# Roots at the head of the step, the FFN bias and the joining of statistics on Vector

## The chip, the cores and the metric

One core of one Trainium2 chip. The metric is the device time of one execution in microseconds, lower is better. The kernel before takes 4009.88 us (median of three runs, 4008.35 to 4010.98).

## What is computed

Sixteen images of 96 channels and 96 x 96 pixels go through two layers. Layer 0 normalises each pixel over its channels, cuts the image into 3 x 3 patches, and for each patch finds the row of a 512 x 96 table and the pixel that match best (a score divided by the pixel's norm); the chosen row, the chosen pixel and the nine similarities of that row go through a small MLP and a convolution and are added to x. A quantised feed-forward network (FFN, 96 to 384 to 96) on the normalised pixels is added to that. Layer 1 divides each normalised pixel by (2 + 1e-4 y)^0.75, where y is the sum of squares over a 5 x 5 window, adds this to x, and adds a second FFN. The part that matters here:

```
def _qlinear(x, W, b):
    y = q_acc(jnp.einsum('bsk,nk->bsn', q_mul(x), q_mul(W)))
    return q_acc(y + q_mul(b))          # q_acc rounds to 10 mantissa bits
def _ln_c(v, eps=1e-6):                 # _gn and _ln_t: the same form, eps 1e-5
    m = jnp.mean(v, axis=1, keepdims=True)
    s = jnp.var(v, axis=1, keepdims=True)
    return (v - m) / jnp.sqrt(s + eps)
```

## The kernel before, in words

A tile is 128 patches (on the partitions) of J = 9 pixels of C = 96 channels; an image is SLOTS = 8 tiles, and there are NT = 128. The kernel is one software pipeline written by hand. In step k each stage works on another tile, by the offsets of `PARTS`: fs (k+4) loads a tile and takes its statistics, f1 (k+3) scores it and selects the pixel, f2 (k+2) finds the table row, f3 (k+1) is the MLP, the convolution and the residual x1, back (k) and tail (k-1) are the first FFN, root2 (k-2) keeps what layer 1 needs, columns and pre (k-10, k-11) apply the window factors, rear and rtail (k-12, k-13) are the second FFN. Each engine's program is one `body(k)`, an order written out by hand; engines meet by semaphores. `steps` unrolls the first 20 steps and the last ones, and runs the images between in a loop whose body is eight steps, one round. In slot 1 of a round GpSimd also prepares the window sums of the image before (`window_parts`) and TensorE makes 26 matmuls of them (`window_sums`); in slot 2 Vector also works out that image's factors (`lrn_columns`).

Four engines share a step. TensorE: nine score matmuls per tile (L422), the MLP, and both FFNs (L392, L399, L407). ScalarE: evicts PSUM (L556), normalises for the FFNs (L590, L604), tanh of the MLP (L646). Vector, in this order: `mlp_input` (L831 to L837); maxima of scores 0 and 1 (`score_max`, L772); `leaky`, the MLP's activation (L842), for which TensorE waits before the next MLP matmul (L451) and ScalarE before its tanh; scores 2 and 3; nine `bn_stats` of the loaded tile (L765); `win_vector` (L817, L821), which gives the table row `vidx`; score 4; nine `bn_stats` of x2; `hidden` of the second FFN (L860, L866); scores 5 and 6; the residual (L850), score 7, nine `bn_stats` of x1, score 8; `hidden` of the first FFN. `bn_stats` leaves count, mean and count x variance of the even and of the odd channels apart. Between these, `run(between)` issues one link at a time of a side chain: from the first score on `pixel_roots` (an inverse root of 128 x 36 numbers per tile: eleven small instructions of 36 elements per partition, nearly all dependent on the one before, and a product of 9; L732 to L757), in the last `hidden` the links of `select` (L782 to L805).

GpSimd, in this order: `ffn_output` for the first FFN (f = y + b2 in f16, L1042, then x2 = x1 + f, L1045) and for the second (the same, for x4); `lrn_rest` (L1066, L1068); `gather` of the table rows by `vidx` (L1023, an indirect DMA); `dot_product` (L1032, L1034); `keep_root2` (L1081 to L1087: five small instructions); `tile_columns` (L1054: four copies); `moments`, which joins the `bn_stats` halves into mean and variance and gives `args` to `pixel_roots` (L999 to L1007, ten instructions of 27 elements or fewer); `gather_pixel` (L1014) by `select`'s `xrow`.

SyncE loads and stores tiles and isn't touched. The two places of the code that set the order around the change, Vector's head and GpSimd's body:

```
run(factors, 1)
if k.f3 is not None:
    mlp_input(k.f3, k.p)
scores(0, 1, 2)          # the last argument: links of `between` after each score
scores(1, 2, 2)
if k.f3 is not None:
    leaky(k.f3)
scores(2, WIN_TURN, 1)
```

## Time and profile before

| | us |
|---|---|
| median of three runs | 4009.88 |
| the profiled execution, its own time | 4034.24 |
| its span in the trace | 4032.4 |

The profiled execution is 24.4 us (0.6%) above the median; 1.8 us of its time lie around the span. A page of the profile gives each engine's busy time; the timeline gives instructions in order of time with their start, their duration, and in brackets how long their engine stood idle before them and what ended that. Neighbouring instructions of a kind are merged into one row (x2, x5). On Vector an instruction can start while the one before it still ends, so what an instruction costs there is the distance between two starts rather than its duration.

### The profile page before, as it was taken

What the parts mean: (1) busy time and instruction counts of PE and PEld (TensorE: products, weight loads), DVE (VectorE), ACT (ScalarE), POOL (GpSimd) and SP (SyncE); (2) the same over time, 40 slices, a digit from 0 to 9 for tenths busy, and PEclk for the clock granted to TensorE, in tenths of its full rate; (3) what the DMA queues carried; (4) which work ended last, traced back from release to release, by engine and by line L of the source; (5) the groups of instructions that cost most, each with busy time, mean ns of one, the idle gap of its engine ahead of it and who ended that gap; (6) DMA issues with size and microseconds to landing.
All of it is one profiled execution on the core that took longest, in us unless ns stands there. A gap on an engine that the chain in (4) does not pass through costs nothing. (4 is left out here: it accounts for less than half of the span.)

```text
span 4032.4 us, 82758 instructions
## 1 busy us (share of the span) xinstructions
PE 3135.5 (78%) x17928; PEld 1696.2 (42%) x17928; DVE 3562.6 (88%) x11127; ACT 2894.7 (72%) x7558; POOL 2575.0 (64%) x3993
## 2 busy tenths in 40 slices
PE   5888878878787877778877787877878877787755
PEld 2444444444444444444444444444444444444432
DVE  6899999898998989999898998989999898999841
ACT  1455878777686777768677686777778777687877
POOL 2555767666666666667666666766667666666654
PEclk9999999999999999999899999999999999999855
DMA  2111111111111111111111111111111111111000
GB/s 76 43 51 33 55 49 56 51 53 49 48 58 45 50 56 46 51 46 55 46 51 55 45 56 46 54 51 50 51 46 55 51 51 50 45 59 45 23 27 36
DMA packets 64738, 197.82 MB, mean 49 GB/s; under 512 B 11391, under 2 KB 14632, under 8 KB 64168
## 3 DMA queue, kind: packets, MB, share of 16 engines
q1 hardware_dynamic: 53928, 172.76, 13.3%
q0 software_dynamic: 10240, 18.89, 1.9%
q8 instruction: 183, 3.00, 0.3%
q14 instruction: 387, 3.17, 0.3%
HBM read 134.60 MB, written 57.02 MB: 48 GB/s over the span
## 5 line engine op out<-in xcount | busy, mean ns | idle before, releaser
L422 PE MATMUL banks<-wcT,xc 128*128 128x512 f32 x2304 | 1246.4, 644 | 184.2 <-DVE mx L772 123.1
L556 ACT ACTIVATE ffn_hid<-banks 128x384 f16<-128x384 f32 x2304 | 1026.9, 487 | 390.2 <-PE banks L399 363.2
L772 DVE TENSOR_REDUCE mx<-banks 128x1 f32<-128x512 f32 x1152 | 775.3, 680 | 114.9 <-PE banks L422 114.0
L399 PE MATMUL banks<-ffn_xT,w1q 128*128 128x384 bf16 x2304 | 690.3, 354 | 182.7 <-ACT ffn_hid L556 137.3
L1042 POOL TENSOR_TENSOR ffn_f<-ffn_y,b2q 128x864 f16<-128x864 f16 x256 | 481.1, 1879 | 229.5 <-ACT ffn_y L556 162.6
L422 PEld LDWEIGHTS banks<-wcT,xc 128*128 128x128 f32 x2304 | 420.8, 202 | 431.5 <-issue 224.9
L399 PEld LDWEIGHTS banks<-ffn_xT,w1q 128*128 128x128 bf16 x2304 | 233.2, 101 | 814.3 <-ACT ffn_hid L556 564.2
L1045 POOL TENSOR_TENSOR x<-x,ffn_f 128x864 f32<-128x864 f32 (+1 forms) x256 | 480.4, 1877 | 62.9 <-POOL ffn_f L1042 62.6
L860 DVE TENSOR_SCALAR ffn_hid<-ffn_hid,b1q 128x1152 f16<-128x1152 f16 x768 | 394.2, 525 | 134.8 <-ACT ffn_hid L556 134.8
L1023 POOL DMA_INDIRECT wrow<-vector_table,vidx x128 | 127.4, 995 | 557.7 <-DVE vidx L821 544.1
L590 ACT ACTIVATE ffn_x<-x,cols 128x96 fp8e5<-128x96 f32 x1152 | 461.1, 456 | 0.0
L590 ACT ACTIVATE ffn_x<-x,nb,roots 128x96 fp8e5<-128x96 f32 x1152 | 425.3, 454 | 27.8 <-DVE nb L757 27.1
L1032 POOL TENSOR_TENSOR prod_dot<-xt,wrow 128x864 f32<-128x864 f32 x128 | 305.2, 2385 | 212.0 <-DMA wrow<-vector_table,vidx 212.0
L556 ACT ACTIVATE ffn_y<-banks 128x480 f16<-128x480 f32 (+1 forms) x512 | 257.9, 531 | 245.8 <-PE banks L407 244.4
L765 DVE BATCH_NORM_STATS2 st<-x 128x6 f32<-128x96 f32 (+1 forms) x2304 | 408.1, 244 | 10.6 <-POOL x L1045 9.4
L556 ACT ACTIVATE ffn_xT<-banks 96x384 bf16<-96x384 f32 x768 | 345.1, 483 | 72.9 <-PE banks L392 37.2
L465 PE MATMUL banks<-wc,h 128*128 128x480 f32 (+1 forms) x1024 | 393.9, 528 | 0.0
L407 PE MATMUL banks<-w2q,ffn_hid 128*128 128x96 bf16 x6912 | 358.6, 212 | 45.4 <-DVE ffn_hid L866 43.0
L407 PEld LDWEIGHTS banks<-w2q,ffn_hid 128*128 128x128 f16 x6912 | 329.0, 102 | 153.0 <-issue 81.9
L392 PE MATMUL banks<-ident_b,ffn_x 128*96 128x128 bf16 x2304 | 227.4, 225 | 177.5 <-ACT ffn_xT L556 149.6
L866 DVE TENSOR_SCALAR ffn_hid<-ffn_hid 128x1152 uint16<-128x1152 uint16 x768 | 338.6, 453 | 0.0
L392 PEld LDWEIGHTS banks<-ident_b,ffn_x 128*96 128x96 fp8e5 x2304 | 176.7, 125 | 291.5 <-issue 282.9
(147 smaller groups left out, 5284.4 us busy)
## 6 DMA issues: line engine op xcount, KB each, us to landing
xt<-x_tok_in SPq DMA_DIRECT2D x128, 432.0 KB, 3.3
xc<-x_chan_in SPq DMA_DIRECT2D x128, 432.0 KB, 4.0
out_tok<-x SPq DMA_DIRECT2D x128, 432.0 KB, 2.5
win<-x_tok_in,xrow POOLq DMA_INDIRECT x128, 2.6
wrow<-vector_table,vidx POOLq DMA_INDIRECT x128, 2.7
shift<-shift_in SPq DMA_DIRECT2D x1, 960.0 KB, 5.0
vector_table<-wtab SPq DMA_DIRECT2D x1, 384.0 KB, 2.9
w1raw<-w_in SPq DMA_DIRECT2D x1, 288.0 KB, 5.8
```

What stands on the lines that cost most here:

```text
L392: last = pe.matmul(bank[0:C, i * P:(i + 1) * P], ffn.x8[:, u * G + i, :], ident_b[:, :], start=True, stop=True)
L399: last = pe.matmul(bank[:, 0:GW], w1q[:, ffn.layer, c * P:(c + 1) * P], ffn.xT[:, g * GW:(g + 1) * GW], start=True, stop=True)
L407: last = pe.matmul(bank[:, (j - j0) * C:(j - j0 + 1) * C], ffn.hid[:, c, j * P:(j + 1) * P], w2q[:, ffn.layer, c, :], start=(c == 0), stop ...
L422: last = pe.matmul(ps_score[score_bank(j)], xc[p][:, j, :], wcT[:, :], start=True, stop=True)
L465: last = pe.matmul(bank[:, 0:(j1 - j0) * C], h1[:, q, :], wc[:, q, j0 * C:j1 * C], start=(q == 0), stop=(q == 1))
L556: return nc.scalar.activation(dst, src, ACT.Copy)
L590: last = nc.scalar.activation(ffn.x8[:, j, :], x[:, j, :], ACT.Identity, bias=bias_c[:, j:j + 1], scale=scale_c[:, j:j + 1], saturate=False)
L765: last = nc.vector.bn_stats(st3[:, which, j, :], src[:, j, :])
L772: nc.vector.tensor_reduce(mx[p][:, j:j + 1], ps_score[score_bank(j)], AX.X, ALU.max).then_inc(score_taken, 1)
L860: nc.vector.tensor_scalar(ffn.hid[:, c, :], ffn.hid[:, c, :], b1q[:, ffn.layer, c:c + 1], 0.0, ALU.add, ALU.max).then_inc(ffn.rounded, 1)
L1042: tt(ffn.f[:, :, :], ffn.y[:, :, :], b2, ALU.add).then_inc(ffn.f_ready, 1)
L1045: tt(dst, x, ffn.f[:, :, :], ALU.add).then_inc(ready, 1)
```

## The change

- GpSimd waits at the head of `body` for `root_ready` of this step, before all of its work.
- Vector issues one link of the roots inside `mlp_input`, and all that remain right behind it; only then come the two bias additions, scores 0 and 1, and `leaky`. The later scores and the first `bn_stats` carry no links any more.
- The bias f = y + b2 (128 x 864, f16) of both FFNs is issued by Vector (`ffn_bias`), once each a step. GpSimd keeps the additions of f to x1 and x3.
- `moments` is on Vector, in seven instructions instead of ten, behind the links of `select`. It leaves twice the mean and the sum of squares, and their users scale by 0.5 and 1/C.
- The statistics stand in one buffer by kind, so `keep_root2` is one copy instead of five instructions, and `tile_columns` one instead of four. The square that `window_parts` needs is made there, once per image, in two instructions of 72 elements.

```diff
-        mom = [sb(f"mom_{i}", [P, 3, J]) for i in range(2)]
-        ss3, var3, mtmp = sb("ss3", [P, 3, J]), sb("var3", [P, 3, J]), sb("mtmp", [P, 3, 3, J])
+
+        pix = [sb(f"pix_{i}", [P, 3, 4, J]) for i in range(2)]
+        twice = [b[:, 0, 0:3, :] for b in pix]
+        ssq = [b[:, 1, 0:3, :] for b in pix]
+        roots = [b[:, 2, :, :] for b in pix]
+        mtmp = sb("mtmp", [P, 2, 3, J])
...
-        mean_i, var_i, rstd_i, sq_i = (sb(n, [P, SLOTS, J]) for n in ("mean_i", "var_i", "rstd_i", "sq_i"))
-        r2 = sb("r2", [P, J])
-
-        cols_i = [sb(f"cols_i{i}", [P, SLOTS, J]) for i in range(4)]
+
+        img = sb("img", [P, 3, SLOTS, J])
+        twice_i, ssq_i, rstd_i = (img[:, i, :, :].rearrange("p s j -> p (s j)") for i in range(3))
+        r2_i, sq_i = sb("r2_i", [P, SLOTS * J]), sb("sq_i", [P, SLOTS * J])
+
+        cols_i = sb("cols_i", [P, 4, SLOTS, J])
...
-                dve.wait_ge(args_ready, k.moments + 1)
+                dve.wait_ge(mom_chain, (k.moments + 1) * MOMENTS)
...
+            MOMENTS = 7
+            mc = Chain(dve, mom_chain, MOMENTS)
+
+            def moments(tile, p):
+
+
+                dve.wait_ge(stats_ready, tile + 1)
+                wait_past(dve, root_ready, tile)
+                wait_past(dve, kept, tile - 6)
+                hold(dve, passed["vector"])
+                mc.begin(tile)
+                of = lambda i: st3[:, :, :, i]
+                d, m2 = mtmp[:, 0, :, :], mtmp[:, 1, :, :]
+                mc.add(nc.vector.tensor_tensor(d, of(1), of(4), ALU.subtract),
+                       nc.vector.tensor_tensor(m2, of(2), of(5), ALU.add))
+                yield
+                mc.wait()
+                mc.add(nc.vector.tensor_tensor(d, d, d, ALU.mult))
+                yield
+                mc.add(nc.vector.tensor_tensor(twice[p], of(1), of(4), ALU.add))
+                yield
+                mc.wait()
+                mc.add(nc.vector.scalar_tensor_tensor(out=ssq[p], in0=d, scalar=C / 4.0, in1=m2, op0=ALU.mult,
+                                                      op1=ALU.add))
+                yield
+                mc.wait()
+                mc.add(nc.vector.scalar_tensor_tensor(out=args[:, 0:3, :], in0=ssq[p], scalar=1.0 / C,
+                                                      in1=eps[:, :, :], op0=ALU.mult, op1=ALU.add),
+                       nc.vector.tensor_copy(args[:, 3, :], ssq[p][:, 1, :]))
+                assert mc.done == mc.per
...
+                f3c.add(nc.vector.tensor_tensor(inp[:, C:D1], dots[:, :], roots[q][:, 3, :], ALU.mult),
+                        nc.vector.tensor_scalar(wnorm[:, :], win[q][:, :], wmean[q][:, 0:1], mix[:, 0:1],
+                                                ALU.subtract, ALU.mult))
+                f3c.wait()
+                run(between, 1)
...
+            def ffn_bias(ffn, tile, added):
+
+                dve.wait_ge(ffn.taken, (tile + 1) * UNITS + 2)
+                wait_past(dve, added, tile)
+                b2 = b2q[:, ffn.layer, :].rearrange("p (o c) -> p o c", o=1).broadcast_to([P, J, C])
+                nc.vector.tensor_tensor(ffn.f[:, :, :], ffn.y[:, :, :], b2, ALU.add).then_inc(ffn.f_ready, 1)
...
-                    mlp_input(k.f3, k.p)
-                scores(0, 1, 2)
-                scores(1, 2, 2)
+                    mlp_input(k.f3, k.p, between)
+                run(between)
+                if k.rtail is not None:
+                    ffn_bias(ffn1, k.rtail, x4_ready)
+                if k.tail is not None:
+                    ffn_bias(ffn0, k.tail, x2_ready)
+                scores(0, 2)
                 if k.f3 is not None:
                     leaky(k.f3)
-                scores(2, WIN_TURN, 1)
+                scores(2, WIN_TURN)
                 if k.fs is not None:
                     dve.wait_ge(xt_loaded[k.p], landed(k.fs, k.p))
                     last = group_stats(1, at(xt, k.fs & XT - 1), between)
                 if k.f2 is not None:
                     win_vector(k.f2, between)
-                run(between)
                 between = factors
...
-                between = select(k.f1, k.p) if k.f1 is not None else iter(())
+                between = chain(select(k.f1, k.p) if k.f1 is not None else (),
+                                moments(k.stats, k.q) if k.stats is not None else ())
                 if k.back is not None:
                     hidden(ffn0, k.back, between)
...
-            MOMENTS = 9
-            mc = Chain(pool, mom_chain, MOMENTS)
-
-            def moments(tile, p):
-
-
-                pool.wait_ge(stats_ready, tile + 1)
-                wait_past(pool, root_ready, tile)
-                mc.begin(tile)
-                of = lambda i: st3[:, :, :, i]
-                t = [mtmp[:, i, :, :] for i in range(3)]
-                mc.link(tt(t[0], of(1), of(4), ALU.subtract), tt(t[1], of(1), of(4), ALU.add),
-                        tt(t[2], of(2), of(5), ALU.add))
-                mc.link(tt(t[0], t[0], t[0], ALU.mult), tt(mom[p][:, :, :], t[1], half[:, :, :], ALU.mult))
-                mc.link(tt(t[0], t[0], c24[:, :, :], ALU.mult))
-                mc.link(tt(ss3[:, :, :], t[0], t[2], ALU.add))
-                mc.link(tt(var3[:, :, :], ss3[:, :, :], inv_c[:, :, :], ALU.mult))
-                hold(pool, passed["pool"])
-                mc.add(nc.gpsimd.tensor_copy(args[:, 3, :], ss3[:, 1, :]))
-                tt(args[:, 0:3, :], var3[:, :, :], eps[:, :, :], ALU.add).then_inc(args_ready, 1)
...
             def ffn_output(ffn, tile, x, dst, ready):
-                pool.wait_ge(ffn.taken, (tile + 1) * UNITS + 2)
-                wait_past(pool, ready, tile)
-                b2 = b2q[:, ffn.layer, :].rearrange("p (o c) -> p o c", o=1).broadcast_to([P, J, C])
-                tt(ffn.f[:, :, :], ffn.y[:, :, :], b2, ALU.add).then_inc(ffn.f_ready, 1)
...
-                for i in range(4):
-                    last = nc.gpsimd.tensor_copy(cols[k.p][:, i, :], at(cols_i[i], k.columns & SLOTS - 1))
-                last.then_inc(cols_ready, 1)
+                nc.gpsimd.tensor_copy(cols[k.p][:, :, :], cols_i[:, :, k.columns_slot, :]).then_inc(cols_ready, 1)
...
-                r2c.begin(k.root2)
-                slot = k.root2 & SLOTS - 1
-                r = roots[k.p][:, 2, :]
-                r2c.add(tt(r2[:, :], r, r, ALU.mult))
-                nc.gpsimd.tensor_copy(at(mean_i, slot), mom[k.p][:, 2, :])
-                nc.gpsimd.tensor_copy(at(var_i, slot), var3[:, 2, :])
-                nc.gpsimd.tensor_copy(at(rstd_i, slot), r)
-                r2c.wait()
+                nc.gpsimd.tensor_copy(img[:, :, k.root2_slot, :], pix[k.p][:, :, 2, :]).then_inc(kept, 1)
+
+            lp = Chain(pool, lrn_pool, 13)
+
+            def window_parts(n):
+
+                lp.begin(n)
+                pool.wait_ge(kept, (n + 1) * SLOTS)
                 hold(pool, passed["pool"])
-                r2c.link(tt(at(sq_i, slot), ss3[:, 2, :], r2[:, :], ALU.mult))
-
-            lp = Chain(pool, lrn_pool, 11)
-
-            def window_parts(n):
-
-                lp.begin(n)
-                s = sq_i[:, :, :].rearrange("p s j -> p (s j)")
-                hold(pool, passed["pool"])
-
-                s3 = s.rearrange("p (m j) -> p m j", j=K)
+                lp.link(tt(r2_i[:, :], rstd_i, rstd_i, ALU.mult))
+                lp.link(tt(sq_i[:, :], ssq_i, r2_i[:, :], ALU.mult))
...
             def body(k):
+                if k.moments is not None:
+
+                    pool.wait_ge(root_ready, k.moments + 1)
                 if k.tail is not None:
                     ffn_output(ffn0, k.tail, x1[k.q][:, :, :], at(x2, k.tail & RING - 1), x2_ready)
...
-                if k.stats is not None:
-
-                    moments(k.stats, k.q)
```

## Rows read from the trace of the kernel before

**Rows 1.** The page: each engine's busy us, share of the span, instructions.

```profile
PE 3135.5 (78%) x17928; PEld 1696.2 (42%) x17928; DVE 3562.6 (88%) x11127; ACT 2894.7 (72%) x7558; POOL 2575.0 (64%) x3993
```

**Rows 2.** Vector's groups by line and form: busy us, mean ns | idle before.

```profile
L743 DVE SCALAR_TENSOR_TENSOR roots<-rtmp,roots 128x36 f32<-128x36 f32 x399 | 261.5, 655 | 4.9
L740 DVE TENSOR_TENSOR rtmp<-rtmp 128x36 f32<-128x36 f32 x399 | 259.5, 650 | 0.5
L737 DVE TENSOR_TENSOR rtmp<-roots 128x36 f32<-128x36 f32 x399 | 252.1, 632 | 4.8
...
L732 DVE TENSOR_SCALAR roots<-args 128x36 int32<-128x36 int32 x133 | 124.2, 934 | 4.1 <-POOL args L1007 3.8
```

**Rows 3.** Vector's timeline, step of slot 4: start us, duration us, engine, line, operation.

```profile
2819.26 0.50 DVE L860 TENSOR_SCALAR ffn_hid<-ffn_hid,b1q 128x1152 f16<-128x1152 f16 x1
...
2820.95 0.59 DVE L831 TENSOR_REDUCE dots<-half_dot 128x9 f32<-128x432 f32 x1
...
2822.44 0.68 DVE L772 TENSOR_REDUCE mx<-banks 128x1 f32<-128x512 f32 x1
2823.04 1.80 DVE L732 TENSOR_SCALAR roots<-args 128x36 int32<-128x36 int32 x1
2824.76 0.17 DVE L733 TENSOR_SCALAR rtmp<-args 128x36 f32<-128x36 f32 x1
...
2825.68 1.32 DVE L740 TENSOR_TENSOR rtmp<-rtmp 128x36 f32<-128x36 f32 x1
2827.04 1.74 DVE L743 SCALAR_TENSOR_TENSOR roots<-rtmp,roots 128x36 f32<-128x36 f32 x1
2828.70 0.54 DVE L842 SCALAR_TENSOR_TENSOR h<-z 96x384 f32<-96x384 f32 x1
```

**Rows 4.** GpSimd's timeline in the same step.

```profile
2821.93 1.02 POOL L1014 DMA_INDIRECT win<-x_tok_in,xrow  x1 [0.46 <-issue]
...
2825.14 1.82 POOL L1045 TENSOR_TENSOR x<-x,ffn_f 128x864 f32 x1 [0.34 <-POOL ffn_f L1042]
```

**Rows 5.** ScalarE's timeline in the same step.

```profile
2816.06 2.33 ACT L556 ACTIVATE ffn_hid<-banks 128x384 f16<-128x384 f32 x5
...
2830.30 0.36 ACT L646 ACTIVATE vcs<-banks,bmlp 96x128 f32<-96x128 f32 x1 [3.00 <-PE banks L451]
```

**Rows 6.** The starts of the MLP's tanh over one round (ScalarE's timeline).

```profile
2643.07 0.36 ACT L646 ACTIVATE vcs<-banks,bmlp 96x128 f32<-96x128 f32 x1 [1.07 <-PE banks L451]
...
2675.45 0.36 ACT L646 ACTIVATE vcs<-banks,bmlp 96x128 f32<-96x128 f32 x1 [1.08 <-PE banks L451]
...
2703.97 0.36 ACT L646 ACTIVATE vcs<-banks,bmlp 96x128 f32<-96x128 f32 x1 [1.07 <-PE banks L451]
...
2738.73 0.36 ACT L646 ACTIVATE vcs<-banks,bmlp 96x128 f32<-96x128 f32 x1 [1.07 <-PE banks L451]
...
2775.49 0.36 ACT L646 ACTIVATE vcs<-banks,bmlp 96x128 f32<-96x128 f32 x1 [3.13 <-PE banks L451]
...
2883.83 0.36 ACT L646 ACTIVATE vcs<-banks,bmlp 96x128 f32<-96x128 f32 x1 [1.07 <-PE banks L451]
```

**Rows 7.** `leaky` by its line: duration ns min/median/max.

```profile
L842 DVE SCALAR_TENSOR_TENSOR h<-z x128: 541/545/2198, 69.1 to 3810.6; 96x384 f32<-96x384 f32 x128
```

**Rows 8.** ScalarE's timeline in the windows' step (slot 1).

```profile
2717.68 0.87 ACT L556 ACTIVATE ffn_hid<-banks 128x384 f16<-128x384 f32 x2 [1.32 <-PE banks L399]
...
2724.39 0.87 ACT L556 ACTIVATE ffn_hid<-banks 128x384 f16<-128x384 f32 x2 [5.49 <-PE banks L399]
```

**Rows 9.** Vector's timeline between `leaky` and the table row, slot 2.

```profile
2738.20 1.20 DVE L737 TENSOR_TENSOR rtmp<-roots 128x36 f32<-128x36 f32 x1
...
2739.93 1.47 DVE L740 TENSOR_TENSOR rtmp<-rtmp 128x36 f32<-128x36 f32 x1
...
2741.50 0.69 DVE L743 SCALAR_TENSOR_TENSOR roots<-rtmp,roots 128x36 f32<-128x36 f32 x1
...
2742.29 0.81 DVE L737 TENSOR_TENSOR rtmp<-roots 128x36 f32<-128x36 f32 x1
```

More of the change, by code:

```diff
@@ L20 @@
 from contextlib import ExitStack
+from itertools import chain
 import numpy as np
@@ L822, in win_vector, with mlp_input @@
                 next(between, None)
-            def mlp_input(f3, q):
+            def mlp_input(f3, q, between):
                 top_q = top[q][:, 0:1]
```

42 lines of the change are left out of this document (18 added, 24 removed).

## The prediction

> **What bounds the kernel now.** I read the page first. Vector is busy 88% of the span, the most of any engine [rows 1], so the next question is what it is busy with. The groups of Vector's instructions show it: the links of the roots take 655, 650, 632 and 934 ns on average for 36 elements [rows 2], while one of them in the timeline takes 0.17 us [rows 3]. By 0.17 us apiece the four groups (399 + 399 + 399 + 133 instructions) would take 226 us; they take 897 us. So 671 us of Vector's "busy" time are stalls.
>
> The timelines say who stalls it. A link starts at 2825.68 and lasts until 2827.00; GpSimd's addition of 864 elements runs from 2825.14 to 2826.96 [rows 3, 4]. The link ends with it. `bn_stats` and the maxima have the same duration beside GpSimd as alone. The Trainium skill gives the reason (SBUF — State Buffer, "SBUF: two separate sides"): a Vector operation with two SBUF inputs or in a two-port mode and a GpSimd operation exclude each other for a whole instruction. The trace agrees.
>
> Then I measured the step. One round of eight steps is 2643.07 to 2883.83, 240.8 us; its steps are 32.4 (slot 7, where the loop branches), 28.5, 34.8 (the windows), 36.8 (the window factors), and 108.3 for the last four, 27.1 each [rows 6]. In the step of slot 4 Vector is full: from 2819.26 to `leaky` at 2828.70 it has no idle time, and ScalarE waits 3.00 us for the matmul behind `leaky` [rows 3, 5]. But a second ring lies close behind Vector. ScalarE finishes the last hidden unit at 2818.39, Vector takes it at 2819.26 (0.83 us late, beside a hop of 0.04), goes through the rest of `hidden`, `mlp_input` and the head to `leaky`, and TensorE and ScalarE follow with the tanh at 2830.30; from a tanh to the last hidden unit ScalarE needs 27.40 - 11.91 = 15.49 us, nearly all of it work [rows 3, 5]. That ring is 26.6 us long. Whatever Vector saves outside it is worth 0.8 us in such a step.
>
> **The change, part by part**, for this step.
>
> *Roots.* Their stalls go: the three stalled links in the head (1.80, 1.32, 1.74 us) and two stalled ones behind `leaky` (1.20 and 0.8 us, as in the like rows of slot 2) are together 6.0 us above 0.17 to 0.20 each [rows 3, 9]. GpSimd starts its long work only after `root_ready`, so no long GpSimd operation can lie beside a root. All twelve now stand ahead of `leaky`, in the ring. Alone, one costs its 0.17 us and 0.04 us to the next (2827.00 to 2827.04 [rows 3]), 0.21 us; ten such links, 0.09 for the independent second and some 0.1 for the last make R = 2.3 us. Bounds: 1.9 (the link inside `mlp_input` hidden) and 3.0 (0.25 each).
>
> *Bias.* The trace has no f16 addition on Vector. The nearest rows are `leaky`, two f32 inputs and 384 elements in 0.54 us [rows 7], and `hidden`'s f16 operation of 1152 in 0.50 us [rows 3]. At the speed of the first 864 elements cost 1.0 us (0.97 from start to start); at the speed of the second 0.4. I take 0.52, between them and nearer the f16 row, so B = 1.04 us for both, bounds 0.8 and 1.94. A page has a rule here: the Trainium skill (VectorE: DVE Perf Modes, "The perf-mode tier table") puts a 16-bit `tensor_tensor` at two elements per cycle, never four; by its 0.96 GHz I estimate 0.45 us plus the fixed part, which gives the same B. What hides the biases from stalls is GpSimd waiting for them.
>
> *Statistics.* Seven instructions of 27 or 9 elements behind `select`, in the ring too. Four dependent ones at 0.21 and three at 0.09 make 1.1; GpSimd's pixel gather (1.02 us [rows 4]) now lies beside them and may stall one, so M = 1.2 us, bounds 1.0 and 2.2. A rule of a page speaks against this part: the Trainium skill (VectorE: DVE Perf Modes, "The TRN2 errata") has a fixed cost for each instruction with SBUF inputs, which many small operations pay many times; the 0.17 us for 36 elements show it here.
>
> *`leaky`.* It stands behind the biases and two maxima, 1.2 us. GpSimd begins x2 about 0.3 us after the second bias (its hop between such instructions is 0.34 [rows 4]) and takes 1.82, so `leaky` finds it running and ends 0.4 us after it, a stall of S = 0.85 us; bounds 0 and 1.65 (2198 - 545 ns [rows 7]). It had stalls before as well, in other slots.
>
> *GpSimd.* It loses two instructions of 1.9 us, ten and seven small ones. It is 64% busy [rows 1], waits for `vidx` each step and stays off the ring, so nothing comes of that by itself. Behind its new wait stand x2 (Vector reads it after score 4, 5 us later), x4 and the rows' gather, which waits for `vidx` anyway. SP's queue moves with x1 and x4 and has slack. The two instructions more per image in `window_parts` are paid from the eight `keep_root2` that shrink.
>
> **The sum of the ring:** ScalarE's 15.49, hop 0.04, rest of `hidden` 1.69 (2819.26 to 2820.95), M 1.2, `mlp_input` 1.49 (to 2822.44), R 2.3, B 1.04, two maxima 1.2, `leaky` 0.54 and S 0.85, to the tanh 1.06: 26.9 us. Vector's own sum is 27.4 - 6.0 (stalls) + 0.7 (roots no longer tucked between other work) + 1.2 + 1.04 + 0.85 = 25.2. So the ring binds, not Vector, and the step gains 0.5 us. Most of the freed time becomes Vector waiting for ScalarE.
>
> **The round.** Slots 3 to 6: 4 x 26.9 = 107.6 for 108.3. Slot 0: 26.9 for 28.5, since its ScalarE waits behind late roots and late maxima go. Slot 7: ScalarE loses 0.57 (its FFN normalisation waiting for the roots) and 1.1 (TensorE behind late maxima, most of the 1.32 in rows 8); the loop's branch stays: 30.7 for 32.4. Slot 1: the same 1.7; the wait of 5.49 us for window matmuls [rows 8] holds 2 us for GpSimd's window parts and some 2 us in which TensorE works slower after that idle time, and both shrink, since `vidx` and the parts come over 3 us earlier: -6.3, +0.8 for a head 0.8 us longer, 29.3 for 34.8. Slot 2: Vector sets it alone, with links of 1.20, 1.47, 0.69 and 0.81 us between `leaky` and the table row [rows 9]; without them and their three short followers it arrives 3.7 us earlier, and the head gains 0.65: 32.4 for 36.8. Sum 226.9 for 240.8: -13.9 us. Over 14.5 rounds of full steps -202; the first twelve steps and the end give some 3 more (the bias after the last matmul is on the end's path: 1.9 us less 0.6). The profiled execution's 4034 would be 3829; the median lies 24 us below it, so **3805 us**.
>
> **Rivals.**
> 1. *The ring is shorter than I think* (chance 0.13). If `leaky` isn't stalled and the small links overlap (S = 0, R = 1.9), the ring is 25.6 and Vector's sum 24: 1.3 us less in seven heads, -9 us per round, -135: 3670 us. For it: 545 ns is the median of `leaky` [rows 7]. Against: GpSimd starts x2 right ahead of it in every step.
> 2. *The head costs more* (0.17). The bias at one element per cycle (+0.9) and a link of `moments` behind the gather (+0.5) are in the ring seven times a round: -4 us a round instead of -14, 3950 us. For it: no row shows the bias.
> 3. *Slower, by the head* (0.07). The place is between `hidden` and `leaky`. M + R + B + S are 5.4 us in the forecast; from 7.4 us on they eat all that the special slots give. With all four at their upper bounds (2.2 + 3.0 + 1.94 + 1.65 = 8.8) each of seven heads is 3.4 us longer than forecast: +10 us a round, 4155 us. Against: four unlikely ends together, and GpSimd's wait keeps the roots clear of its long operations.
> 4. *It does not do what it says* (0.05). If GpSimd's gathers, not its additions, held the roots, the stalls would stay in the new place, and what the bias leaves cancels what it costs: 4005 us. Against: the ends at 2827.00 and 2826.96 agree.
>
> **How the numbers follow.** My forecast holds 0.58. Range 3690 to 3950: it leaves out a bit of the first rival, the outer half of the second, and the third and fourth. A difference of 0.2% (8 us) is about what can be told from no change here. Faster by more: 0.58 + 0.13 + 0.17 = 0.88; within 0.04; slower 0.08.
>
> **What would show it.** Root links of 0.17 to 0.2 us on average, one after the other; two f16 additions of 864 elements on Vector near 0.6 us long; ScalarE's 3.00 us wait at the tanh down to 2.5 or so, and new idle time of Vector before its last hidden unit (L860) of about 1 us a step; `leaky` at 1.2 to 1.4 us; plain steps of 26.9 us, the windows' step under 30, the factors' near 32. I am wrong if the plain step is under 26 (then the ring isn't what I hold it to be) or over 27.4, or if the round's gain comes from the plain steps rather than from slots 1, 2 and 7.

## The result, and the profile after

The changed kernel takes 4130.48 us (median of four runs, 4128.91 to 4134.11) against 4010.43 us for the kernel before on the same chip: ratio 1.0293, interval 1.0280 to 1.0305. The forecast was 3805 us, range 3690 to 3950. The change makes the kernel 3% slower, on the side to which the prediction gave 0.08. The two profiled executions lie only 99.9 us apart (4132.3 and 4032.4), since that of the kernel before is 24 us above its median; what is read from the traces below adds up to that.

The page of the profiled execution (span 4132.3 us) shows that the parts did what they say. Busy us, share of the span, instructions, to be held against [rows 1]:

```profile
PE 3283.0 (79%) x17928; PEld 1795.2 (43%) x17928; DVE 3336.1 (81%) x12311; ACT 2906.4 (70%) x7558; POOL 1540.8 (37%) x1543
```

Vector, with 1184 instructions more, is busy 226 us less, GpSimd 1034 us less. TensorE has the same 17928 matmuls and is busy 148 us more. Groups of instructions by line (busy us, mean ns of one | idle time before them and what ended it):

```profile
L429 PE MATMUL banks<-wcT,xc 128*128 128x512 f32 x2304 | 1384.1, 707 | 252.2 <-DVE mx L808 209.8 <-issue 38.0 <-ACT wc L563 2.4
L808 DVE TENSOR_REDUCE mx<-banks 128x1 f32<-128x512 f32 x1152 | 774.9, 684 | 358.8 <-PE banks L429 346.9
...
L881 DVE SCALAR_TENSOR_TENSOR h<-z 96x384 f32<-96x384 f32 x128 | 179.3, 1400 | 2.7 <-ACT z L643 2.7
L922 DVE TENSOR_TENSOR ffn_f<-ffn_y,b2q 128x864 f16<-128x864 f16 x256 | 145.2, 605 | 29.6 <-ACT ffn_y L563 27.2
L744 DVE TENSOR_TENSOR rtmp<-rtmp 128x36 f32<-128x36 f32 x399 | 78.1, 196 | 13.6
```

A root link now takes 196 ns instead of 650 [rows 2]: that stall is gone. The f16 bias is 605 ns, `leaky` (L881) 1400 ns, both as forecast. The two rows not forecast are the first ones. The score matmuls (L429) take 707 ns each, 644 before, and stand idle 210 us for a maximum, 123 before. The maxima (L808) stand idle 347 us for scores, 114 before.

The distance between starts of the MLP's tanh says in which steps the time went (us, median over the rounds; the mean of 13 whole rounds is 241.0 before and 245.8 after). Slots 3 to 6 are the plain steps; the first steps are the twelve at the start, in which the second FFN has no work yet:

| slot | 7 | 0 | 1 | 2 | 3 | 4 | 5 | 6 | the first steps |
|---|---|---|---|---|---|---|---|---|---|
| before | 33.3 | 29.2 | 31.8 | 36.8 | 27.4 | 27.4 | 27.4 | 26.1 | 24.0 |
| after | 31.2 | 29.8 | 30.9 | 34.5 | 30.0 | 30.3 | 30.3 | 29.0 | 27.3 |

The special slots 7, 1 and 2 gained, as forecast. Every plain step lost 2.6 to 2.9 us. By stretches of the span, up to the 13th tanh the kernel loses 35 us, up to the 26th 19, from there to the last tanh 52; the end gains 7. More than a third of the 100 us is lost in the first twelve steps.

One plain step (the tanh at 2887.01 to the one at 2917.30), TensorE's timeline:

```profile
2904.76 1.31 PE L414 MATMUL banks<-w2q,ffn_hid 128*128 128x96 bf16 x27
2907.71 0.36 PE L446 MATMUL banks<-ident,inp 128*105 128x128 f32 x1 [1.65 <-DVE inp L876]
...
2909.87 0.27 PE L435 MATMUL banks<-ident,win 128*96 128x128 f32 x1
2911.61 2.08 PE L429 MATMUL banks<-wcT,xc 128*128 128x512 f32 x2 [1.47 <-DVE mx L808]
2913.48 0.85 PE L406 MATMUL banks<-ffn_xT,w1q 128*128 128x384 bf16 x2
2914.12 1.92 PE L429 MATMUL banks<-wcT,xc 128*128 128x512 f32 x2
2915.83 1.44 PE L458 MATMUL banks<-h,wi 96*96 96x128 f32 x6
```

And Vector's:

```profile
2904.64 0.21 DVE L779 TENSOR_TENSOR mtmp<-st 128x27 f32<-128x27 f32 x1
...
2905.75 0.59 DVE L867 TENSOR_REDUCE dots<-half_dot 128x9 f32<-128x432 f32 x1
...
2907.58 0.18 DVE L741 TENSOR_TENSOR rtmp<-pix 128x36 f32<-128x36 f32 x1
...
2909.83 1.13 DVE L922 TENSOR_TENSOR ffn_f<-ffn_y,b2q 128x864 f16<-128x864 f16 x2
2910.88 1.28 DVE L808 TENSOR_REDUCE mx<-banks 128x1 f32<-128x512 f32 x2
2912.07 1.44 DVE L881 SCALAR_TENSOR_TENSOR h<-z 96x384 f32<-96x384 f32 x1
2913.73 0.69 DVE L808 TENSOR_REDUCE mx<-banks 128x1 f32<-128x512 f32 x1 [0.22 <-PE banks L429]
2916.07 0.69 DVE L808 TENSOR_REDUCE mx<-banks 128x1 f32<-128x512 f32 x1 [1.65 <-PE banks L429]
```

`leaky` ends at 2913.51, but the matmul that wants it (L458) starts at 2915.83. What keeps it is TensorE's own queue: ahead of L458 stand score 2, two hidden units of the second FFN (L406) and score 3. Score 2 takes the bank that the maximum of score 0 frees, and that maximum now stands behind roots and biases. It lets score 2 go at 2911.61, after 1.47 us idle. This holds for nearly all steps: in the kernel before the matmul behind `leaky` (L451 there) waited for it 119 times in 128, 170.1 us in all; in the changed kernel it (L458) did so 3 times, 5.9 us in all. And then the queue runs slowly: a score (the x2 pair of one 128x512 matmul) takes 2.08 us, 1.02 at other times. The windows of this stretch (us; busy PE, PEld, DVE, ACT, POOL; then the granted clock, DMA share, GB/s):

```profile
2905.00:2908.00 3.00, 1.35 (x27) 1.11 (x24) 2.65 (x15) 1.44 (x4) 0.41 (x1) 1.00 0.08 16
2908.00:2910.00 2.00, 1.57 (x17) 1.32 (x16) 1.71 (x9) 1.75 (x5) 0.00 (x0) 1.00 0.04 8
2910.00:2912.00 2.00, 0.53 (x3) 0.39 (x2) 2.00 (x4) 1.16 (x5) 0.72 (x1) 0.57 0.00 0
2912.00:2914.00 2.00, 2.00 (x4) 0.61 (x4) 1.78 (x3) 0.00 (x0) 2.00 (x2) 0.50 0.00 0
2914.00:2916.00 2.00, 2.00 (x5) 0.92 (x4) 0.42 (x1) 1.22 (x3) 1.98 (x2) 0.50 0.00 0
```

The granted clock goes from 1.00 to 0.50, from 2.4 to 1.2 GHz, while TensorE stands idle for the second time within 6 us, and stays there until the queue has reached L458, which itself takes 1.44 us for 0.87. The plain step of the kernel before has 1.00 throughout:

```profile
2802.90:2830.30 27.40, 22.22 (x138) 12.05 (x136) 27.11 (x84) 22.55 (x60) 19.71 (x30) 1.00 0.18 56
```

The same was read in 95 steps of each trace, from the 25th tanh to the 119th: the pair of score 2, 1.02 to 1.13 us at the full clock, takes over 1.3 us in 81 of the 95 steps of the changed kernel and in 5 of the kernel before. So the step has a late start of the queue and a slow run of it, and the experiments are to divide the blame.

### The profile page after: what moved, and what is told of

Read it like the earlier page. It is cut to its first block and busy times, and to the rows that moved or that the text cites. A ratio compares the mean times of both kernels' runs of the same rounds, so it can differ in the third digit from the quotient of the medians.

```text
span 4132.3 us, 80817 instructions
## 1 busy us (share of the span) xinstructions
PE 3283.0 (79%) x17928; PEld 1795.2 (43%) x17928; DVE 3336.1 (81%) x12311; ACT 2906.4 (70%) x7558; POOL 1540.8 (37%) x1543
## 5 line engine op out<-in xcount | busy, mean ns | idle before, releaser
L429 PE MATMUL banks<-wcT,xc 128*128 128x512 f32 x2304 | 1384.1, 707 | 252.2 <-DVE mx L808 209.8
L808 DVE TENSOR_REDUCE mx<-banks 128x1 f32<-128x512 f32 x1152 | 774.9, 684 | 358.8 <-PE banks L429 346.9
L406 PE MATMUL banks<-ffn_xT,w1q 128*128 128x384 bf16 x2304 | 712.7, 364 | 182.9 <-ACT ffn_hid L563 137.2
L1069 POOL TENSOR_TENSOR x<-x,ffn_f 128x864 f32<-128x864 f32 (+1 forms) x256 | 496.6, 1959 | 915.3 <-DVE ffn_f L922 827.2
L429 PEld LDWEIGHTS banks<-wcT,xc 128*128 128x128 f32 x2304 | 463.5, 220 | 523.4 <-DVE mx L808 269.1
L406 PEld LDWEIGHTS banks<-ffn_xT,w1q 128*128 128x128 bf16 x2304 | 240.5, 105 | 845.1 <-ACT ffn_hid L563 589.5
L597 ACT ACTIVATE ffn_x<-x,nb,pix 128x96 fp8e5<-128x96 f32 x1152 | 425.1, 457 | 0.0
L1042 POOL DMA_INDIRECT win<-x_tok_in,xrow x128 | 129.6, 1013 | 695.0 <-DVE xrow L831 667.4
L611 ACT ACTIVATE x<-x,cols 128x96 f32 (+1 forms) x640 | 293.6, 461 | 0.4 <-POOL cols L1077 0.4
```

Of the source, the lines that this page charges most:

```text
L406: last = pe.matmul(bank[:, 0:GW], w1q[:, ffn.layer, c * P:(c + 1) * P], ffn.xT[:, g * GW:(g + 1) * GW], start=True, stop=True)
L429: last = pe.matmul(ps_score[score_bank(j)], xc[p][:, j, :], wcT[:, :], start=True, stop=True)
L597: last = nc.scalar.activation(ffn.x8[:, j, :], x[:, j, :], ACT.Identity, bias=bias_c[:, j:j + 1], scale=scale_c[:, j:j + 1], saturate=False)
L808: nc.vector.tensor_reduce(mx[p][:, j:j + 1], ps_score[score_bank(j)], AX.X, ALU.max).then_inc(score_taken, 1)
L1069: tt(dst, x, ffn.f[:, :, :], ALU.add).then_inc(ready, 1)
```

## The experiments

The expectations speak of **theory A** (TensorE's queue: what stands ahead of L458 waits for the late maximum 0), **theory B** (Vector's head itself, with the stall of `leaky` by GpSimd's x2) and **theory C** (the lower clock level behind the idle time multiplies the delay). Ratios are to the kernel before on the same chip, which took 4012.8 to 4027.9 us. The changed kernel varies less from chip to chip than that (4130.48 us above, and 4130.30 in the run below without GpSimd's wait, whose ratios are 1.0293 and 1.0251), so a difference of less than 0.005 between two ratios says little.

**Maxima first.** The changed kernel with

```diff
+                scores(0, 2)
                 run(between)
                 if k.rtail is not None:
                     ffn_bias(ffn1, k.rtail, x4_ready)
                 if k.tail is not None:
                     ffn_bias(ffn0, k.tail, x2_ready)
-                scores(0, 2)
                 if k.f3 is not None:
                     leaky(k.f3)
```

> The changed kernel, with Vector's maxima of scores 0 and 1 put back right behind the MLP input, ahead of the roots and the two biases. Theory A (what was lost is TensorE's queue: score 2, the first hidden units of the second FFN and score 3 stand ahead of the MLP's middle matmul, and score 2 waits for Vector's maximum of score 0, which now comes 3.2 us later): the wait of the score matmuls for the maxima (210 us in the changed kernel) falls under 60, a plain step from 30.0 to about 26.3 us, since leaky also stands ahead of GpSimd's addition then and isn't stalled (545 ns); total about 3720 us. Theory B (the ring ScalarE, Vector, leaky is simply longer by the roots, biases and moments): Vector's work up to leaky is the same, so only leaky's stall of 0.85 us goes; plain step 29.2, total about 4020. Theory C (TensorE's lower granted clock, 0.881 against 0.928, is a cause of its own): the clock stays under 0.89 and the time over 4050.

3865.87 us, ratio 0.9604 (0.9586 to 0.9623), between what A (3720) and B (4020) gave. Plain steps 27.5 us. Moving 1.2 us of work by 3.3 us on one engine is worth 265 us against the changed kernel. It also lets `leaky` follow the biases at once, ahead of x2 (0.55 us, no stall), so that A, B and C are not yet apart.

**TensorE's order instead**: L458 ahead of score 2, score 3 last.

```diff
-                scores(2, 3)
                 hidden_units(ffn1, k.rear, 0, 2)
-                scores(3, WIN_TURN)
...
                     mlp_mid(k.f3)
+                scores(2, 3)
                 hidden_units(ffn1, k.rear, 2, 2)
                 if k.f3 is not None:
                     mlp_last(k.f3)
+                scores(3, WIN_TURN)
```

> The changed kernel, Vector untouched; on TensorE score matmuls 2 and 3 are put behind the MLP's middle matmul (score 2 right behind it, score 3 behind the MLP's last one). Theory A: the middle matmul then follows leaky at once, the tanh comes 2 us earlier, and part of that is lost again since the two scores now lie in front of the later MLP matmuls: plain step 28 to 28.7, total 3900 to 4000. Theory B: TensorE's order is indifferent, within 30 us of 4130. Theory C: no gain unless the clock rises.

4329.71 us, ratio 1.0754 (1.0729 to 1.0779): a miss, slower still. From TensorE's timeline, and from Vector's one step earlier:

```profile
3063.76 0.87 PE L458 MATMUL banks<-h,wi 96*96 96x128 f32 x6 [3.18 <-DVE h L881]
```
```profile
3035.80 0.69 DVE L808 TENSOR_REDUCE mx<-banks 128x1 f32<-128x512 f32 x1 [2.78 <-PE banks L429]
3038.23 0.69 DVE L808 TENSOR_REDUCE mx<-banks 128x1 f32<-128x512 f32 x1 [1.74 <-PE banks L429]
```

With L458 first, its wait for `leaky` (3.18 us idle) holds scores 2 and 3, and Vector stands idle 4.5 us for them behind `leaky` (2.78 and 1.74); before its step had no such gap. Theory A had looked at the MLP's chain alone. What waits at the head of a queue is paid by everything behind it, in either order.

**The kernel before with late maxima:**

```diff
-                scores(0, 1, 2)
-                scores(1, 2, 2)
+                run(between, 4)
+                scores(0, 2)
```

> The kernel before, with Vector's four first root links issued ahead of the maxima of scores 0 and 1 instead of between them, so that both maxima stand right ahead of leaky; no work is added. Theory A: TensorE gets score 2 some 3 us later, and its three pieces of work in front of the middle matmul end after leaky: plain step 27.4 to 29.0 or more, total 4120 to 4200. Theory B: the same work up to leaky, so the time stays at 4010 within 15.

4050.14 us, ratio 1.0055 (1.0035 to 1.0076), less than A's 4120 and a little more than B's 4010. In the full steps the total says little, since the reordering also takes stalls out of the head: a plain step is 27.3 us for 27.4, and score 2 waits only 0.94 us there. The first twelve steps, which have no second FFN, say more: 27.2 us instead of 24.0, as in the changed kernel (27.3). There TensorE waits 2.71 us for the maximum and then runs two scores in 3.54 us, which take 1.88 at other times:

```profile
228.71 3.54 PE L422 MATMUL banks<-wcT,xc 128*128 128x512 f32 x4 [2.71 <-DVE mx L772]
```

In these steps the loss can be made in the kernel before with none of the change's new work.

**Biases back on GpSimd**, behind its new wait:

```diff
-                    ffn_bias(ffn1, k.rtail, x4_ready)
-                    ffn_bias(ffn0, k.tail, x2_ready)
...
             def ffn_output(ffn, tile, x, dst, ready):
+                tt(ffn.f[:, :, :], ffn.y[:, :, :], b2, ALU.add).then_inc(ffn.f_ready, 1)
```

> The changed kernel with both bias additions back on GpSimd behind its wait for the roots; the rest as changed. Theory A and B both: the maxima and leaky come 1.05 us earlier, so a plain step loses about 1 us: 29.0, total about 4020. Rival: leaky, now beside GpSimd's f16 addition from its start, is stalled by up to 1.65 us and the gain is eaten: 4100 to 4150.

3896.98 us, ratio 0.9687 (0.9667 to 0.9707), 233 us less than the changed kernel, where 110 were expected. Two things changed at once: 1.05 us of Vector's work, and the stall of `leaky`, which is gone too (median 556 ns for 1433). Together they are some 1.9 us a step, over 127 steps some 245, so the total alone doesn't tell whether something multiplies the delay. The plain step does: it is 27.3 us for 30.3, 2.9 less, and `leaky` is not what ends last in it:

```profile
2736.05 1.62 PE L429 MATMUL banks<-wcT,xc 128*128 128x512 f32 x2
2736.99 0.55 DVE L881 SCALAR_TENSOR_TENSOR h<-z 96x384 f32<-96x384 f32 x1 [0.79 <-ACT z L643]
2738.69 0.82 PE L458 MATMUL banks<-h,wi 96*96 96x128 f32 x6
```

`leaky` ends at 2737.54 and L458 starts 1.15 us later, behind the queue. Against the changed kernel score 2 starts 0.8 us earlier after the tanh, the queue from it to L458 is 1.6 us shorter (2.64 for 4.22), and L458 itself takes 0.6 us less.

**Three matmuls more in each idle time** of TensorE (their results are never read; a wait that guards the PSUM they write stands ahead of them), ahead of the wait for the MLP's input and ahead of score 2:

```diff
+                wait_past(pe, x1_ready, f3)
+                for _ in range(3):
+                    pe.matmul(ps_a[:, :], ident[:, :], wcT[:, :], start=True, stop=True)
                 pe.wait_ge(inp_ready, f3 + 1)
-                wait_past(pe, x1_ready, f3)
...
+                if k.f3 is not None and k.tail is not None:
+                    pe.wait_ge(ffn0.taken, (k.tail + 1) * UNITS + 2)
+                    for _ in range(3):
+                        pe.matmul(banks[:, ffn0.bank, :], ident[:, :], wcT[:, :], start=True, stop=True)
                 scores(2, 3)
```

> The changed kernel, its order untouched; TensorE makes six extra 128x512 matmuls a step whose results nobody reads, three before it waits for the MLP input and three before it waits for the maximum of score 0 (PSUM that is free then). In the changed kernel it stands idle there for 1.65 and 1.47 us and its next matmuls take twice as long (2.08 us for a score pair of rows, against 1.02). Theory A+C (the queue in front of the middle matmul costs so much because it runs at the lower clock level): the clock rises from 0.881 to over 0.95, score 2 to middle matmul shrinks from 4.2 to about 2.2 us, plain step 30.1 to 28.1, total about 3880 to 3930. Theory A alone (the queue, whatever the clock): the extra matmuls only add work, 4130 or a little more.

4123.97 us, ratio 1.0247 (1.0230 to 1.0264), for 3880 to 3930 by A and C: inconclusive. The score pair is back at 1.02 us, but the three take 2.7 us, longer than the gaps of 1.65 and 1.47, and what they give they take by making the queue late. The same ahead of the input only, in the version with maxima first:

> The run with the maxima first (3866 us), with three extra matmuls, which nobody reads, before TensorE's wait for the MLP input. Theory A+C: the same effect as a shorter idle time, plain step 27.4 to about 26.5, total about 3740 to 3770, clock from 0.91 to over 0.95. Theory A alone: 3866 or slower.

3839.11 us, ratio 0.9541 (0.9525 to 0.9557), 27 us less than without them, where some 110 were expected.

**One matmul in each place**, which fits the gaps (both times, against the three):

```diff
-                for _ in range(3):
+                for _ in range(1):
```

> The changed kernel with one more 128x512 matmul on TensorE (its result is never read) ahead of the wait for the MLP's input and one ahead of score 2: 0.4 to 0.87 us each, shorter than the idle times of 1.65 and 1.47 us that they stand in, so that nothing queued behind them is late, as it was with three. Theory C (the lower clock level behind the idle time multiplies the delay): the granted clock of the step rises, the score pair takes nearer 1.0 than 2.1 us, the plain step loses 1.5 to 2 us: 3920 us, ratio 0.975. Theory A without C (the wait itself, not the clock behind it): 4130 us, ratio 1.03.

3909.20 us, ratio 0.9714 (0.9697 to 0.9731): theory C. The kernel's own work and its order are unchanged, only TensorE has more to do, and it is some 5% faster than the changed kernel (3909.20 us for 4130.48). TensorE's timeline (L528 is the new matmul) and the windows:

```profile
2745.35 1.02 PE L528 MATMUL banks<-wcT,ident 128*128 128x512 f32 x2
2746.98 1.12 PE L429 MATMUL banks<-wcT,xc 128*128 128x512 f32 x2 [0.61 <-DVE mx L814]
2747.95 0.49 PE L406 MATMUL banks<-ffn_xT,w1q 128*128 128x384 bf16 x2
2748.27 1.02 PE L429 MATMUL banks<-wcT,xc 128*128 128x512 f32 x2
2749.13 0.82 PE L460 MATMUL banks<-h,wi 96*96 96x128 f32 x6
```
```profile
2745.00:2747.00 2.00, 1.39 (x8) 0.56 (x6) 1.97 (x5) 1.52 (x6) 0.36 (x1) 1.00 0.00 0
2747.00:2749.00 2.00, 2.00 (x6) 0.83 (x7) 2.00 (x3) 0.69 (x2) 2.00 (x2) 1.00 0.00 0
```

Maximum 0 is as late as ever, and Vector's rows are those of the changed kernel, `leaky`'s stall (1.44 us) with them. But score 2, L406 and score 3 now take 2.15 us to pass, not 4.2, and L460 (L458 there) starts 0.25 us after `leaky` ends. The plain step is 27.6 us instead of 30.3, and in none of the 95 steps does score 2 take over 1.3 us.

**Only the one ahead of score 2:**

> The changed kernel with one matmul more ahead of score 2 only; the idle time of 1.65 us ahead of the MLP's input stays, as the kernel before has it. If the idle time ahead of score 2 is what brings the clock down: granted clock 1.00 in plain steps, 27.6 us each, as with both matmuls: 3910 to 3930 us, ratio 0.975. If both idle times have an equal share: about half of the gain, 4020 us, ratio 1.00. If the first does it: 4130 us.

3937.32 us, ratio 0.9782 (0.9764 to 0.9800); plain steps 27.6 us, with a granted clock of 1.00 in the one that was read. The idle time of 1.64 us ahead of the MLP's input stays and costs the plain step nothing. It does cost elsewhere: in the first twelve steps the matmuls of the input behind it (L451) mostly take 1.59 us for 0.90, and these steps stay at 27.2 us, where matmuls in both places make them 25.2. Of the 26 us between the two traces 14 lie there. **The other one, in the kernel before:**

> The kernel before with one matmul more ahead of the wait for the MLP's input. Its plain steps have the granted clock 1.00 already, so they keep their 27.4 us; the matmul delays the transpose of the input by 0 to 0.2 us. Only the steps of the windows and the factors can gain, 0 to 4 us a round: 3970 to 4030 us, ratio 0.985 to 1.00. If that idle time cost clock in the kernel before too, it would gain as the changed kernel did, 220 us: 3800 us, ratio 0.945.

4024.25 us, ratio 0.9991 (0.9981 to 1.0001), plain steps 27.4 us. So in the full steps it is the new one of the two gaps, ahead of score 2, whose filling keeps the clock up: score 2 takes over 1.3 us in 13 of the 95 steps with it filled, in 81 without.

**Where the head has to be cut.** One maximum first, the other behind the biases:

```diff
+                scores(0, 1)
                 run(between)
...
-                scores(0, 2)
+                scores(1, 2)
```

> The changed kernel with only the maximum of score 0 ahead of the roots; that of score 1 stays behind the two biases. `leaky` still comes late enough behind the second bias to meet GpSimd's x2. Theory A (TensorE's queue: score 2 stands ahead of the middle MLP matmul and waits for maximum 0): score 2 and the two hidden units behind it run during the roots, score 3 starts when maximum 1 is there, and the MLP matmul starts when the stalled `leaky` ends, some 2 us earlier than in the changed kernel: 3900 us, ratio to before 0.97. Theory B (the stall of `leaky` and Vector's own head set the step, not the queue): nothing changes, 4130 us, ratio 1.03.

4015.83 us, ratio 0.9977 (0.9966 to 0.9987), between A (3900) and B (4130). In the plain step that was read (28.1 us, median 28.5) the granted clock is 1.00: score 2 fills the gap. What ends last now is `leaky`:

```profile
2823.15 2.03 DVE L881 SCALAR_TENSOR_TENSOR h<-z 96x384 f32<-96x384 f32 x1
2823.29 1.13 PE L429 MATMUL banks<-wcT,xc 128*128 128x512 f32 x2 [0.88 <-DVE mx L808]
2825.33 0.87 PE L458 MATMUL banks<-h,wi 96*96 96x128 f32 x6 [0.92 <-DVE h L881]
```

It now starts one maximum earlier behind the biases, just after GpSimd has begun x2, and so is stalled longer (median 2033 ns for 1433), and L458 waits for it 122 times in 128. With the queue out of the way theory B's stall is what the step pays. Then both maxima between roots and biases:

```diff
                 run(between)
+                scores(0, 2)
...
-                scores(0, 2)
                 if k.f3 is not None:
                     leaky(k.f3)
```

> The changed kernel with both maxima between the roots and the biases. `leaky` now follows the biases at once, ahead of GpSimd's x2, so that its stall of 0.9 us goes, and maximum 0 comes 1.05 us earlier. Theory A (TensorE's queue alone): the step is 1.05 us shorter, some 120 us in all: 4010 us, ratio 1.00. Theory B (the stall alone): 0.9 us a step, 4030 us, ratio 1.003. If the lower level of TensorE's clock behind its idle time multiplies the delay: over 2 us a step, 3900 us or less, ratio 0.97.

3895.44 us, ratio 0.9678 (0.9659 to 0.9697), plain steps 27.3 us: the third outcome, 2.9 us a plain step for 1.05 us of delay and 0.9 us of stall (`leaky` takes 547 ns). As in the run with the biases on GpSimd the queue still ends after `leaky`; L458 waits for it 7 times in 128.

**GpSimd's wait taken out:**

```diff
             def body(k):
-                if k.moments is not None:
-
-                    pool.wait_ge(root_ready, k.moments + 1)
```

> The changed kernel without GpSimd's wait for the roots at its head. GpSimd's first work waits for Vector's bias, which stands behind the roots in Vector's own order, so the wait holds nothing more: 4130 us, ratio 1.03. If the second FFN's or any other long GpSimd operation then meets the roots: links of over 1 us in the profile, 4150 us or more.

4130.30 us, ratio 1.0251 (1.0234 to 1.0268), spans equal to 0.1 us: it has no share, since x2 waits for Vector's bias, which stands behind the roots.

**Towards a faster version.** From maxima first, the moments moved out of the last `hidden` of the step before:

```diff
-                between = pixel_roots(k) if k.moments is not None else iter(())
+                between = (chain(moments(k.moments, k.p), pixel_roots(k)) if k.moments is not None
+                           else iter(()))
```

> The run with the maxima first (3866 us), with the seven moments instructions moved from the end of Vector's step to behind the next step's MLP input and maxima, ahead of the roots. The MLP input comes 1.1 us earlier against the last hidden unit, TensorE idles 0.5 us before its transpose instead of 1.65. Theory A+C: the clock stays up in the head (input matmuls 0.85 instead of 1.54 us, score pair 1.02 instead of 1.90), plain step 27.4 to about 26.3, total about 3720. Theory A alone: the same work on Vector up to leaky, so 3866 within 20.

3866.03 us, ratio 0.9606 (0.9590 to 0.9622): nothing gained, for the 3720 expected. Then also both biases behind `leaky`:

```diff
+                if k.f3 is not None:
+                    leaky(k.f3)
                 if k.rtail is not None:
                     ffn_bias(ffn1, k.rtail, x4_ready)
                 if k.tail is not None:
                     ffn_bias(ffn0, k.tail, x2_ready)
-                if k.f3 is not None:
-                    leaky(k.f3)
```

> Candidate: maxima first, moments behind the MLP input, then the roots, then leaky, and the two biases behind leaky, where Vector used to wait for scores 2 and 3. The ring ScalarE, Vector, leaky loses the biases too (1.05 us) and GpSimd's additions begin behind leaky, so it can't be stalled by them. By theory A+C the ring is 25.0 us and Vector's own sum about 24.5: plain step 25.2, total about 3560 to 3620. Rival: what GpSimd begins later (x2, x4, the gather) becomes late itself, and the time stays at that of the run with the moments moved.

3709.41 us, ratio 0.9216 (0.9201 to 0.9231), the fastest so far, if not the 3560 to 3620 expected. `leaky` also ahead of the last root links:

```diff
-                run(between)
+                run(between, 11)
                 if k.f3 is not None:
                     leaky(k.f3)
+                run(between)
```

> The version with maxima first, moments behind them, biases behind `leaky` (3709 us), and now `leaky` itself ahead of the last four links of the roots, at about the time when ScalarE hands it its input. Theory A: the MLP's ring is 0.7 us shorter, plain step 25.2 us, 3620 us, ratio 0.90. If ScalarE's own work (some 24.5 us a step in a row) already binds: 3690 to 3710, ratio 0.92.

3707.96 us, ratio 0.9212 (0.9196 to 0.9227): no difference. ScalarE has 22.6 us of work in a plain step of 25.9 and short waits between; that it sets the step is likely by that, but no run shows it. And the fastest version without the move of the moments, so with nothing but the head's order changed:

> The changed kernel with nothing moved but pieces of Vector's head: maxima of scores 0 and 1, roots, `leaky`, then both biases; the moments stay behind `select`. If the order of the head is the whole cause: as fast as the version that also moved the moments, 3700 to 3730 us, ratio 0.922. If the moments' place matters once the biases are out of the way (they then stand ahead of the MLP's input again, 1.1 us in the ring): 3780 to 3830 us, ratio 0.945.

3853.58 us, ratio 0.9600 (0.9578 to 0.9623), slower than either outcome: the moments' place does matter. From maxima first (0.9604), the move of the moments alone gives 0.9606, that of the biases alone 0.9600, no difference that can be told; both together give 0.9216, some 156 us. Each alone leaves one of two limits. With the moments ahead of the MLP's input, the clock falls behind that wait, and L458 waits for TensorE's queue (for `leaky` 3 times in 128):

```profile
2696.85 0.36 PE L446 MATMUL banks<-ident,inp 128*105 128x128 f32 x1 [1.64 <-DVE inp L876]
...
2698.33 1.41 PE L451 MATMUL banks<-inpT,wi 105*96 105x128 f32 x6
2699.53 0.42 PE L435 MATMUL banks<-ident,win 128*96 128x128 f32 x1
2699.74 1.91 PE L429 MATMUL banks<-wcT,xc 128*128 128x512 f32 x2
```

With the moments moved and the biases still ahead of `leaky`, the matmuls from the input to score 3 run at full speed, but then TensorE stands idle for `leaky` (124 times in 128), 1.89 and 1.71 us in two steps in a row. Behind the first of them the clock is 0.60, and a pair of 128x512 matmuls (L441) takes 1.91 us for 1.02:

```profile
2686.70 0.87 PE L458 MATMUL banks<-h,wi 96*96 96x128 f32 x6 [1.89 <-DVE h L881]
...
2688.90 1.91 PE L441 MATMUL banks<-wcT,winT 128*128 128x512 f32 x2
...
2715.61 0.87 PE L458 MATMUL banks<-h,wi 96*96 96x128 f32 x6 [1.71 <-DVE h L881]
```

With both moves, a plain step is 25.9 us. The fastest version with one matmul more ahead of the MLP's input:

> The version with maxima first, moments behind them and both biases behind `leaky` (3709 us), with one matmul more ahead of the wait for the MLP's input. Its plain steps already show the granted clock 1.00 and full-speed matmuls, so they stay at 25.9 us; what the special steps lose to the clock may come back, 1 to 2 us a round: 3680 to 3700 us, ratio 0.917. If the matmul is late for the input's transpose: 3720 us.

3714.83 us, ratio 0.9220 (0.9205 to 0.9236): nothing. Where no clock is lost, filling an idle time gives nothing back; with the same result in the kernel before, that is the control for theory C.

## Why the prediction was wrong

**Roots: right.** 194 to 196 ns a link, one after the other; from the first full row (2907.58) to the bias 2.25 us for R = 2.3.

**Bias: right.** 1.05 us for both (2909.83 to 2910.88), B = 1.04. Rival 2's bias at the slower speed did not come. The rule cited for it (the Trainium skill, VectorE: DVE Perf Modes, "The perf-mode tier table") agrees with the trace: 605 ns for 864 f16 elements, where `leaky`, with two f32 inputs, takes 550 ns for 384.

**Statistics: right.** M = 1.2; measured 1.11 (2904.64 to 2905.75). The gather at 2904.40 to 2905.41 lies beside the moments and stalls none of them.

**`leaky`'s stall: right.** S = 0.85, measured 0.89 (1.44 less 0.55).

**The ring's own length: a little short.** From tanh to Vector's last hidden unit 15.98 us instead of 15.53, `mlp_input` with its two root instructions 1.83 instead of 1.49. By the forecast's sum with these terms the tanh would come 1.06 after `leaky`'s end at 2913.51, at 2914.57: a step of 27.6 us for the 26.9 forecast. The kernel with one matmul more in each gap shows just that, 27.6, and a mean round of 231.9 for the 226.9 forecast. This error alone would have left the forecast right in sign, at a ratio near that kernel's 0.971 (0.949 was forecast).

**The step that failed** is "the sum of the ring", in the item *two maxima, 1.2 us*. It counted them as Vector's work on the way to `leaky`, and asked only when `leaky` ends. But the maxima also free TensorE's score banks, and score 2, two hidden units and score 3 stand in TensorE's queue ahead of the matmul that wants `leaky`. The change puts roots and biases, 3.3 us, ahead of the maxima. In the kernel before maximum 0 stands at 2822.44 [rows 3], right behind the MLP's input, so that this queue was through at 2827.1 and TensorE then waited 2.34 us for `leaky`. This slack was in the trace and was not read:

```profile
2826.03 1.02 PE L422 MATMUL banks<-wcT,xc 128*128 128x512 f32 x2
2829.39 0.87 PE L451 MATMUL banks<-h,wi 96*96 96x128 f32 x6 [2.34 <-DVE h L842]
```

The delay of the maxima uses up this slack and hardly more. With the queue at full speed it would have cost the plain step 0.1 us: in the kernel with one matmul more, where maximum 0 is as late, the matmul starts 0.25 us after `leaky` ends, and 0.15 us after it in the kernel before. It costs 30.29 - 27.56 = 2.7 us since behind the idle time ahead of score 2 TensorE runs at the lower clock level just where its queue has become the path. The sum had no term for this: it took TensorE's part as the 1.06 us from `leaky` to the tanh.

**Slots**: 7, 1 and 2 were to gain 1.7, 5.5 and 4.4 us; by the medians they gained 2.1, 0.9 and 2.3, slots 1 and 2 with the same loss inside them. With one matmul in each gap they are 29.2 and 32.5 us, for the 29.3 and 32.4 forecast. But the one round that the prediction read was untypical in slot 1: 34.8 us there, 31.8 in the median round.

**The rivals.** The third had the sign and nearly the time (4155 us), but by a head of 8.8 us; the head's four parts measured 5.3 of the 5.4 forecast, so it is wrong as a mechanism. Its chance was small because only lengths on Vector were priced, not what TensorE has queued behind them. The prediction saw TensorE slower after idle time in slot 1 and gave it 2 us back there; it never asked where the change makes a new idle time.

**Signs it had named**: a plain step over 27.4 us and the missing of new idle time on Vector ahead of its last hidden unit; the idle time came ahead of scores 2 and 3 instead (347 us in all).

What is not settled is when a gap brings the clock down. The one ahead of the input has a median of 1.6 us in six of these kernels, and the matmuls behind it (L451, 0.85 us at the full clock) take over 1.2 us in 14 of the 95 steps of the changed kernel and 12 with one matmul ahead of score 2, but in 59 with maxima first, 53 with the biases on GpSimd, 49 with the maxima between roots and biases, and 52 with the head's order changed alone. In these four the matmuls are slow already ahead of score 2, so a gap there is not needed for it. Yet TensorE's rows in the 5 us up to the gap are alike in the steps that were read with the head's order changed alone (1.41 us for L451) and with one matmul ahead of score 2 (0.85). No run tells that apart.

## What to carry to other kernels

When a change moves a consumer (here a maximum that frees a PSUM bank), read the other engine's queue from the instruction that it releases to the next one on the path, and count the slack that stood between. Count each new idle time of TensorE by what the matmuls behind it take at half the clock, if they are on the path; one matmul of no use, short enough for the gap, tests this in a single run. Two limits of about equal length hide each other: here two moves gave nothing alone, and some 156 us together. And when a run takes two costs away at once, as the biases and the stall of `leaky`, look in its trace at which of them ended last before crediting either.

## What the runs showed of the hardware

An added matmul can make a kernel faster: two per step, 269 us of TensorE's busy time in all, took some 220 us off. The lower level of the clock shows at 2910 to 2916 us, behind idle times of 1.65 and 1.47 us with 2.4 us between them, 0.43 of which were idle too. A single idle time of 2.34 us ahead of L451 in the kernel before left it at 1.00, while behind one of 1.6 us ahead of the input it fell in about half of the steps of other kernels (53 of 95 with the biases on GpSimd). The length of an idle time alone does not tell. The Trainium skill (TensorE: Matmul & The Clock Gate, "A second HAM failure mode: psum-queue depth-cycling") has a like case: in a kernel that cycles through PSUM banks, short idle times between groups of matmuls make the clock swing between its two levels. The trace agrees: the wait of 1.47 us is one for a PSUM bank, and the clock in the windows is 1.00 before it and 0.50 behind it, with 0.57 where it changes.
